# Pair-table blocks fetched one turn ahead in a four-layer graph kernel: a wait moved to VectorE, a reduce split into two additions, group stores issued later

## The reference

```python
temp = segment_sum(vals[:, None] * wx[col], row)                  # layer 0
agg  = segment_sum(concat([x[row], edge_attr]) @ W1 + b1, col)    # layer 1
agg  = segment_sum(w[:, None] * x[src], dst)                      # layer 2, twice
t    = einsum('nd,kod->kno', h, W_et) + b_et[:, None, :]          # layer 3, three steps
a    = segment_sum(t[etypes, src], dst);  h = gru_cell(a, h, ...)
```

## Time and profile before

| | us |
|---|---|
| median of 3 runs | 14650.35 |
| lowest, highest | 14632.92, 14655.12 |
| the profiled execution: its own time | 14650.93 |
| the profiled execution: its span | 14649.3 |
| mean granted TensorE clock in it | 0.780 of 2.4 GHz |

### The profile page before, as it was taken

One profiled execution on the slowest core, in us unless ns is written; L12 is line 12 of the kernel. 1 busy time (PEld: TensorE's weight loads), 2 busy tenths in 40 slices (PEclk: granted clock), 3 DMA queues, 4 the chain that ended last, 5 costly groups with the idle time before them and its releaser, 6 DMA issues. The chain is left out here.

```text
span 14649.3 us, 174126 instructions
## 1 busy us (share of the span) xinstructions
PE 9259.6 (63%) x36994; PEld 6192.8 (42%) x36995; DVE 7129.5 (49%) x20949; ACT 1463.7 (10%) x4222; POOL 9840.9 (67%) x8999
## 2 busy tenths in 40 slices
PE   5343444444446777756664555579995999778885
PEld 3333333433443555544443333334443444434442
DVE  3333333333346777568885777543333333333333
ACT  1111111111110000000000000010000000000001
POOL 2777777777783766757775666637774777657771
PEclk6666666776778888766776666689997999899996
DMA  9989997777769888668884888569993899568872
GB/s 293 217 214 217 217 216 158 167 163 160 134 90 231 211 210 208 152 164 226 226 213 125 206 206 206 139 209 255 253 253 95 248 253 252 167 173 226 226 213 68
DMA packets 4146178, 2879.06 MB, mean 197 GB/s; under 512 B 441509, under 2 KB 3854754, under 8 KB 4145798
## 3 DMA queue, kind: packets, MB, share of 16 engines
q1 hardware_dynamic: 3596044, 2237.34, 55.3%
q0 software_dynamic: 518096, 623.51, 21.9%
q10 hardware_dynamic: 31722, 15.04, 0.4%
HBM read 2113.07 MB, written 790.78 MB: 198 GB/s over the span
## 5 line engine op out<-in xcount | busy, mean ns | idle before, releaser
L989 POOL DMA_INDIRECT ring<-t_types,stage x3456 | 3306.2, 957 | 1584.5 <-issue 1510.5
L1527 PE MATMUL bank<-ring 128*128 128x128 f32 x13824 | 2390.7, 330 | 1371.8 <-DMA ring<-t_types,stage 484.9
L1527 PEld LDWEIGHTS bank<-ring 128*128 128x128 f32 x13824 | 2174.4, 237 | 2263.9 <-issue 1863.5
L989 POOL DMA_INDIRECT ring<-t_x,stage x2304 | 2252.5, 978 | 1128.7 <-issue 943.8
L1996 DVE TENSOR_REDUCE work<-work 128x512 f32<-128x2048 f32 x588 | 2147.6, 3652 | 824.5 <-DMA work<-t_pairs 823.3
L1505 PE MATMUL bank<-work 128*128 128x512 f32 x4704 | 2149.0, 600 | 84.2 <-DMA work<-t_pairs 58.9
L948 POOL DMA_INDIRECT t_sums<-ring,stage x1152 | 1784.1, 1549 | 581.7 <-issue 253.2
L1975 DVE TENSOR_TENSOR acc<-acc,bank 128x128 f32 x1728 | 486.2, 281 | 2333.5 <-PE bank L1527 2273.9
L989 POOL DMA_INDIRECT ring<-t_h,stage x1152 | 1089.0, 945 | 617.3 <-issue 416.7
L1414 PE MATMUL bank<-aux 128*128 128x128 f32 x2304 | 528.0, 401 | 1308.4 <-ACT aux L1118 1307.9
L1505 PEld LDWEIGHTS bank<-work 128*128 128x128 f32 x4704 | 857.9, 192 | 959.3 <-issue 884.6
(11 more groups left out here) (304 smaller groups left out, 11171.3 us busy)
## 6 DMA issues: line engine op xcount, KB each, us to landing
work<-t_pairs SPq DMA_DIRECT2D x2352, 512.0 KB
t_pairs<-acc SPq DMA_DIRECT2D x272, 740.0 KB
aux<-sorted_src SPq DMA_DIRECT2D x400, 256.0 KB
t_pairs<-acc SPq DMA_DIRECT2D x78, 1300.0 KB
t_pairs<-acc SPq DMA_DIRECT2D x272, 370.0 KB
t_types<-work SPq DMA_DIRECT2D x156, 512.0 KB, 6.6
work<-t_types SPq DMA_DIRECT2D x294, 256.0 KB
ring<-t_types,stage POOLq DMA_INDIRECT x3456
```

The costliest lines, as they stand in the source:

```text
L989: pool.indirect_dma_start(msg[:, u, :], None, table, bass.IndirectOffsetOnAxis(ap=stage[:, u:u + 1], axis=0)).then_inc(slot_dma[u], 16)
L1527: mm = pe.matmul(bank[q][:, 0:P], msg[:, u, :], hot[:, u, :], start=k_ == 0, stop=k_ == K - 1)
```

## The change

1. A block's place is given back by VectorE in passes 1 to 3 for both halves: the load of unit u waits for S(u-2), never for B(u-2). The 64 KB source tile behind the block of half 0 gets a wait of its own, until TensorE has done unit u-5 (`dense_done >= unit - 4`), in those passes.
2. In pass 1 SyncE issues the three blocks of turn t+1 among the features of turn t, where it issued those of turn t. The first three blocks of the pass stand ahead of everything.
3. In all passes `store(p - 2)` is issued between turn 2p and turn 2p+1, not before turn 2p.
4. `type_sums` is two additions, with a semaphore between, and not one reduce.

```diff
@@ unit_rows
-                wait(sp, types_summed if ph < 4 and half else dense_done,
-                     unit - 1 if not isinstance(p, int) or unit > 1 else 0)
+                wait(sp, types_summed if ph < 4 else dense_done, unit - 1 if not isinstance(p, int) or unit > 1 else 0)
...
                 if half == 0:
+                    if ph < 4:
+                        wait(sp, dense_done, unit - 4 if not isinstance(p, int) else (ph - 1) * UNITS)
                     sp.dma_start(dense_t[:, tile, :] if ph > 3 else dense_x[:, tile, :], table[at, :]
@@ stream_pass
                         if a == 0 and not (isinstance(p, int) and p == 0):
                             load(p - 1)
-                            if not (isinstance(p, int) and p == 1):
-                                store(p - 2)
+                        if a == 1 and not (isinstance(p, int) and p < 2):
+                            store(p - 2)
...
+                        def next_unit(i):
+                            if a == 0:
+                                if TILES + i < units:
+                                    unit_rows(ph, table, p, TILES + i)
+                            elif not isinstance(p, int) or p < LEAD:
+                                unit_rows(ph, table, p + 1, i)
                         if ph == 1:
-                            features_in(p * 2 + a, unit)
+                            features_in(p * 2 + a, next_unit)
...
+                if ph == 1:
+                    for i in range(TILES):
+                        unit_rows(ph, table, 0, i)
                 pairs_of_turns(sp, body)
@@ type_sums
-                    v.tensor_reduce(dense_sum[:, half, :], dense_b[:, half, :, :].rearrange("p (k b) c -> p (b c) k", k=KT),
-                                    AXIS.X, ALU.add).then_inc(types_summed, 1)
+                    two = [dense_b[:, half, i * 8:i * 8 + 8, :].rearrange("p b c -> p (b c)") for i in range(2)]
+                    v.tensor_tensor(two[0], two[0], two[1], ALU.add).then_inc(types_halved, 1)
+                    v.wait_ge(types_halved, unit + 1)
+                    v.tensor_tensor(dense_sum[:, half, :], two[0][:, 0:GN], two[0][:, GN:2 * GN], ALU.add
+                                    ).then_inc(types_summed, 1)
```

More of the change, by code:

```diff
@@ L299, in build @@
         dense_x_in = [sem(f"dense_x_in{i}") for i in range(TILES)]
+        types_halved = sem("types_halved")
         types_summed = sem("types_summed")
```

## The result

The changed kernel takes 15504.0 us (median of 4 runs, 15496.3 to 15510.5) where the kernel before takes 14649.7 (4 runs): ratio 1.0585, 95% interval 1.0567 to 1.0603. The profiled execution has a span of 15506.9 us, 857.6 more than before, at a mean granted clock of 0.764. The forecast was 14765, with a range that ended at 14900. The sign was right and the size was more than seven times too small (+115 us forecast, +854 measured).

The account below looks back on a forecast made before the run. GpSimd's gathers were taken to bound passes 2 and 4 to 6, VectorE's lateness adding stalls in 1 and 3. 14650.9 + 122 (pass 1) + 88 (pass 2) - 94 (pass 3) + 0 = 14767, forecast 14765, range 14580 to 14900.

Parts of the forecast that it names:

- Free: Store's move behind three blocks: VectorE needs its buffer some 20 us on, against 6.6 for a block, so no cost.
- the prediction's own rule: Passes 2 and 4 to 6 go at GpSimd's pace, one gather in 1.25 us; another engine's savings cannot show.
- passes 4 to 6 unchanged: Sign named in advance: the change adds 0 us to passes 4 to 6.
- features behind blocks: Pass 1: features wait behind blocks and type sums, a pair of turns goes from 46.2 to 50.0 us, +122 us.
- Rival B: Pass 1: features get through in time, -52 there, total 14593, faster; chance 0.10.
- additions hold gathers: Passes 2 and 3: VectorE's two-operand additions delay GpSimd's gathers, 88 us for 196 type sums in each pass.
- My 0.45: Gather time in us lost per type sum, from the formula's 0.49 scaled by 0.11 / 0.13.
- The formula: A gather beginning x into an addition is held for the addition's length - 0.13 - x.
- rival A: Type sums: additions don't hold gathers, total 14591, faster; decided if the hold is under 0.2 us a sum; chance 0.13.
- the 182 us of stalls: Pass 3: GpSimd's waits for ScalarE's index copies beyond issue gaps, all forecast to go; with +88 that gives -94.
- Rival D: Pass 3: the stall stays since ScalarE still waits for moments hanging on TensorE's products, total 14949; chance 0.06.
- Its own range: The forecast case's range, 14680 to 14870: pass 1 pair 48 to 53 us, hold 0.25 to 0.7 us a sum.

Follow-up runs that it names:

- the half blocks: Kernel before with half of each pair-table block left out in passes 2 to 6, 0.9965; additions added 0.9799, late store in passes 4 and 5 1.0071, whole change 0.9892.

## Why the prediction was wrong

**The step that failed.** "The store passes three blocks in SyncE's queue; VectorE next needs its buffer in turn 2p+1, some 20 us on, against 6.6 for a block. Free." Two things are wrong in it. First, I asked who needs the buffer next for one kind of pass and wrote the answer for all six. In passes 4 and 5 the stored types lie in memory that ScalarE's gates overwrite; line 1253 says so, `wait(act, types_out[1], gates.out(i))`, and it wasn't read as a consumer. The gates come while TensorE is still in turn 2p: in the kernel before they run at 10337.44, 13.1 us after the store's issue at 10324.33. Second, I set one block's 6.6 us against the time left, but three blocks stand ahead of the store, each with a wait for its own place. Its issue fell behind the gates' due time: 10346.46 against 10338.9. The runs with the store behind one, two and three blocks show the slack, on slower chips: one is free, two are nearly so, three are not. And behind a late gate stands what the prediction's own rule asks for, the index copies and with them GpSimd, which had no stall in that pass. The new term is +370 and +376 where the sum had 0. Of the signs that the prediction named, "passes 4 to 6 unchanged" is the one that failed. The sign came out for a part of the reason given: passes 1 to 3 alone make +92 us.

Why it costs 370 us a pass on the first chip and 169 to 177 on the others is not fully settled. With the late store pass 4 takes 1826 us on the first and 1895 to 1926 on the others, so 50.7 us a pair and 52.6 to 53.5; with the early store 1456 and 1726 to 1758, 40.4 a pair and 47.9 to 48.8. A loop through the late store that is about equally long everywhere fits: the first chip has more to lose because it was faster without it. That is an argument from lengths; the runs meant to restore its balance did not, and with half the bytes the loop shrank to 50.1.

**Pass 1: features behind blocks.** The mechanism was right, the size somewhat too large. The pitch is 48.5 us, where 50.0 was forecast from 46.2; the waits for features rose from 83.5 to 238.2, and vanish when the order is taken back. The pass grew by 77 us and not 122, as the pitch has it: (48.5 - 46.2) x 32 is 74. That type sums lie in the loop is borne out by the variant with the reduce kept, +146 us. Rival B ("features get through in time") is out.

**Pass 2: additions hold gathers.** Right: +96 for +88 forecast. The mean gather is 1193.50 / 1152 = 1.036 us, 0.948 before; 101 us over 196 sums is 0.52 a sum where I took 0.45. My 0.45 had a slip in it: (1104.1 - 1089.0) / 132 divides by all the additions of pass 4, though pass 3 has 33 of its own. By the 99 that differ it is 0.15 each, and 0.49 scaled by 0.15 / 0.13 gives 0.57. The formula held for the addition of 1024: begun 0.54 into 1.22 us, 0.94 + 1.22 - 0.13 - 0.54 = 1.49, and the row says 1.50. One begun with it comes to 2.03 by it, 2.05 in the row. The 96 gathers of the pass that began 0.1 to 0.9 us into a first addition ended 0.82 us behind it in the mean, which is what the earlier trace rows gave. The additions alone raise the mean gather, so it is neither the place nor the store. The Trainium skill (SBUF — State Buffer, Who interferes with whom) has two sentences on this. By the first, a VectorE instruction with two SBUF inputs contends with GpSimd's reads, and the trace agrees, 2.05 against 0.94 us. By the second, a tensor_tensor had not stalled a DMA issued by GpSimd in a probe; here it does stall an indirect one, and rival A, whose sum that sentence would give, is out: the hold is 0.52 us a sum, where A needed under 0.2.

**Pass 3.** Right: the 182 us of stalls are gone, GpSimd waits 18.9 us in 62 issue gaps, and what is left is the 101 us of held gathers: -81 for -94. Rival D is out. The variant with the reduce kept adds that on its chip the pass falls from 1937 to 1715 us without the additions, and with the additions alone only to 1845. So there the additions were not needed for what they were credited with; whether the first chip's 182 us would have gone without them wasn't run. Under GpSimd's pace they cost 96 us in pass 2, and in pass 3 the gathers' busy time rose by 1190.46 - 1088.99, 101 us.

**The range.** It was built on costs that I had found and mis-sized, and had no case for one that I had priced at nothing. I named the cover of the store's move, but not what it would cost if the cover was gone: behind three blocks the store leaves 20.6 us later against TensorE's product (12.9 us ahead of its end before, 7.7 behind it after), in two more passes. Its own range of 14680 to 14870 was also narrower than its ends added up, 14625 to 14961.

## What to carry to other kernels

When a transfer is moved back in a queue, list every engine that waits for its semaphore, in each pass that runs the code, and read from the timeline when the first of them comes; a buffer reused by another engine waits as hard as the owner does. Compare the slack with all that now stands ahead, not with one transfer. Move such a statement only in the passes where it pays: on the slower chips the same move is worth 1.2 per cent in passes 1 to 3 and costs 2.2 in passes 4 and 5.

If GpSimd issues the gathers and sets the pace, a reduce of one operand can be better than two additions that take half the time: in pass 2 on the first chip the additions came with 96 us more, and the engine that they relieved wasn't the one that set the pace. And a ratio from one chip need not hold on another: the whole change is 1.0585 on one and 1.0026 on another.

## What the runs showed of the hardware

The chips differ, and the time is not in the transfers or the gathers. What stands ahead of pass 1 takes as long everywhere: its first gather is at 4570 and 4583 us on the first chip and at 4556 to 4584 on the others. In pass 6 GpSimd is busy 1103.32 us on the first chip (the changed kernel) and 1103.87 on another (the store behind one block), in passes of 1455 and 1738 us, and a gather's last packet ends 2.4 and 2.1 us behind its instruction in the median. What differs are the moments at which other engines go on after TensorE. Take ScalarE's index copies of pass 6 before which it stood for 0.15 us or more. In the changed kernel on the first chip (234 copies) the copy starts 0.13 us behind the end of TensorE's last sum in the median and at the 95th percentile. The same program on a slower chip (169) has a median of 0.95 us, and one copy in twenty comes 6.8 us and more behind; the variant with the store behind one block (179) has 0.41 and 7.2. There is a place in that variant's pass where it is seen:
```profile
14538.09 1.95 PE L1529 MATMUL bank<-ring 128*128 128x128 f32 x16
...
14540.47 3.70 PE L1507 MATMUL bank<-work 128*128 128x512 f32 x8 [0.43 <-issue]
...
14544.01 0.94 PE L1529 MATMUL bank<-ring 128*128 128x128 f32 x7
...
14545.32 0.57 ACT L1193 ACTIVATE stage<-meta_row 128x4 uint32 x3 [10.60 <-remote]
14545.41 0.29 DVE L1977 TENSOR_TENSOR acc<-acc,bank 128x128 f32 x1 [8.69 <-remote]
14545.50 1.78 SPq L650 DMA_DIRECT2D work<-t_types  x1
14546.33 0.97 POOL L991 DMA_INDIRECT ring<-t_types,stage  x1 [3.41 <-ACT stage L1193]
```
Two sums end at 14540.0 by the records, but ScalarE makes three copies in one go at 14545.32, VectorE goes on at the same moment, and GpSimd has stood for 3.41 us. Either TensorE's signals reach the others late, or its sums really end later than the modelled ends say. The records of semaphore events are sparser in these traces ("remote" is a wait whose releaser isn't in them), so which of the two it is stays open, and so does its cause. That it is not the bytes of the blocks was shown by the half blocks. Nor is it shown that the chip itself is the cause, rather than something else that differed between these hours.
